# Attention in a four-layer kernel: the running maxima placed along a concave line, and the second one of a place put behind the values

## What is computed

```python
# 16 heads of 16 channels, 2048 queries and keys, causal
attn = jnp.einsum('bhqd,bhkd->bhqk', q, k) / math.sqrt(HEAD_DIM)
attn = attn + alibi_bias(seq_len, N_HEADS)[None] + causal_mask(seq_len)[None, None]
attn = jax.nn.softmax(attn, axis=-1)
y = jnp.einsum('bhqk,bhkd->bhqd', attn, v)
...
x = x + _L0_attn_ref(_layernorm(x, axis=-1), L0_attn_W_qkv, L0_attn_W_o)
...
x = x + _L1_attn_ref(_layernorm(x, axis=-1), L1_attn_Wq, ...)   # rotary instead of ALiBi
```

## Time and profile before

| | |
|---|---|
| Median of the runs shown | 1660.2 us |
| The profiled execution's own time | 1662.96 us |
| Span of its profile | 1661.2 us |
| Granted TensorE clock, mean of the span | 0.945 |
| Places of the first attention (0 to 319) | 233.0 to 674.1 us of the span |
| Places of the second attention | 1040.8 to 1496.9 us of the span |

### The profile page before, as it was taken

The page is one execution under the profiler, slowest core; times in us unless marked ns, Lnnn a source line. Parts: engine busy times, 40 slices in busy tenths (PEclk is TensorE's granted clock), DMA queues, the critical chain, the costliest instruction groups (busy, mean ns, idle before and its releaser), DMA issues. The chain is left out here.

```text
span 1661.2 us, 32231 instructions
## 1 busy us (share of the span) xinstructions
PE 1511.0 (91%) x13116; PEld 946.3 (57%) x13116; DVE 1242.6 (75%) x1741; ACT 945.3 (57%) x1893; POOL 207.6 (12%) x275
## 2 busy tenths in 40 slices
PE   2798888989999999999899698899999999998997
PEld 0687754444434445688688676544344344456887
DVE  7765457888898883576589887677788988735897
ACT  5454334757768887565344322456577688863442
POOL 0243000000000000157000033000000001220000
PEclk9899968999999999999999898789799999999999
DMA  6000869000000000200100067841110000000000
GB/s 218 26 0 9 176 169 130 25 21 25 15 14 14 2 2 2 77 1 1 39 1 1 1 138 205 104 59 45 39 33 25 13 12 2 2 1 1 13 13 26
DMA packets 38195, 70.58 MB, mean 42 GB/s; under 512 B 5490, under 2 KB 13298, under 8 KB 37236
## 3 DMA queue, kind: packets, MB, share of 16 engines
q1 hardware_dynamic: 38052, 68.58, 18.4%
HBM read 48.90 MB, written 22.15 MB: 43 GB/s over the span
## 5 line engine op out<-in xcount | busy, mean ns | idle before, releaser
L1362 DVE TENSOR_REDUCE l_att_maxima<-psum 128x2 f32<-128x1024 f32 (+3 forms) x640 | 664.8, 1063 | 137.1 <-PE psum L1154 128.6
L1547 ACT ACTIVATE l_att_probs<-psum 128x512 f32<-128x512 f32 (+3 forms) x1280 | 603.6, 533 | 263.4 <-PE psum L1184 242.7
L1201 PE MATMUL psum<-l_att_probs,l_att_v 128*17 128x256 f32 (+2 forms) x4608 | 352.7, 383 | 0.5
L1184 PE MATMUL psum<-l_att_qt,l_kt 51*128 51x512 f32 (+6 forms) x1280 | 319.6, 461 | 6.6 <-ACT l_att_probs L1547 6.6
L1154 PE MATMUL psum<-l_kt,l_att_qt 59*128 59x512 f32 (+7 forms) x1280 | 287.6, 427 | 4.6 <-DVE l_att_maxima L1362 3.0
L1184 PEld LDWEIGHTS psum<-l_att_qt,l_kt 59*128 59x128 f32 (+1 forms) x1280 | 138.0, 192 | 156.1 <-ACT l_att_probs L1547 146.1
L1201 PEld LDWEIGHTS psum<-l_att_probs,l_att_v 128*17 128x17 f32 x4608 | 81.9, 96 | 143.1 <-issue 92.2
L1154 PEld LDWEIGHTS psum<-l_kt,l_att_qt 59*128 59x128 f32 (+1 forms) x1280 | 140.5, 202 | 18.8 <-DVE l_att_maxima L1362 17.4
L358 PE MATMUL psum<-xh,w_ternary 128*128 128x512 f32 x256 | 103.7, 405 | 21.0 <-PEq L165 16.3
L1502 POOL CAST l_att_crow<-l_att_cneg 128x16 bf16<-128x16 f32 x32 | 8.1, 252 | 802.4 <-DVE l_att_cneg L1372 802.4
L1151 PE MATMUL psum<-tri 64*128 64x128 bf16 x1024 | 89.2, 239 | 20.1 <-DVE l_att_maxima L1362 13.7
(11 more groups left out here) (209 smaller groups left out, 2507.0 us busy)
## 6 DMA issues: line engine op xcount, KB each, us to landing
l_kt<-qk_scratch SPq DMA_DIRECT2D x48, 256.0 KB, 10.2
qk_scratch<-l_att_kv_parts SPq DMA_DIRECT2D x22, 512.0 KB, 8.1
l_att_qt<-qk_scratch SPq DMA_DIRECT2D x168, 64.0 KB
qk_scratch<-y SPq DMA_DIRECT2D x10, 512.0 KB, 12.5
set_raw<-in_w_gu SPq DMA_DIRECT2D x2, 1024.0 KB, 7.0
y<-in_w_gu SPq DMA_DIRECT2D x1, 2048.0 KB, 7.6
y<-in_rope SPq DMA_DIRECT2D x8, 256.0 KB, 5.9
l_att_w_raw<-in_w_gu SPq DMA_DIRECT2D x4, 512.0 KB
```

The source lines that it names most:

```text
L1184: e.matmul(g.ps[:, score_bank(i), off:BLK], g.kt[rows_of(x), hp, kt * P:(kt + 1) * P], qt[rows_of(x), hp, off:BLK], start=u >= TPB, stop=True,
L1201: ins = e.matmul(g.ps[h * VW:h * VW + HD + 1, OB, lo:hi], g.v[:, kt, STEPS[st][1] * HG + h, :], pr[:, un % PB, h, lo:hi], start=u == 0 and ...
L1362: e.tensor_reduce(mp[:, st % 2, 2 * p:2 * p + 2, t, c], g.ps[:, bank:bank + 2, 0:w], AX.X, ALU.max).then_inc(s.mx, 1)
L1547: e.activation(pr[:, un % PB, h, off:BLK], g.ps[:, score_bank(i), off:BLK], ACT.Exp, scale=HD ** -0.5).then_inc(s.ex, 1)
```

## The change

The corners stay; what runs between them changes. Up to corner (16, 32) the straight lines are kept. From there on, `due` is the largest value that any chord between two of the later corners has at that place, that is, the concave line over the corners. It touches them at (16, 32), (24, 48), (88, 120), (184, 224) and (280, 320) and lies above the others. Between 24 and 88 it rises by 72 products in 64 places, between 88 and 184 by 104 in 96, and then by one for each place. So two products stand at places 16 to 23, then at 24, 32, 40, 48, 56, 64, 72, 80, 88, then at 100, 112, 124, 136, 148, 160, 172; all other places up to 279 have one. The number of places with two is 24, as before; the maxima run up to six products ahead of the old line.

The second part is `due_first`: the first product of a place stands where it stood, and a second one stands behind rows, output and values of that place. VectorE and ScalarE count the ring in the same new order. Sizes, banks, rings, waits and the places of rows, outputs and values are as before.

```diff
+        corners = [(maxima_place(st), mbase[st + 1]) for st in range(NS)]
+
         def due(p):
 
-            for st in range(NS):
-                end = maxima_place(st)
-                if p < end:
-                    begin = maxima_place(st - 1)
-                    return mbase[st] + -(-(mbase[st + 1] - mbase[st]) * (p - begin) // (end - begin))
-            return mbase[NS]
+            for (a, c), (b, d) in zip(corners[:NG - 1], corners[1:NG]):
+                if p < b:
+                    return c + -(-(d - c) * max(0, p - a) // (b - a))
+            late = corners[NG - 1:]
+            return max([-(-((d - c) * (p - a) + c * (b - a)) // (b - a)) for a, c in late for b, d in late if a <= p < b],
+                       default=mbase[NS])
+
+        def due_first(p):
+
+            return min(due(p) + 1, due(p + 1))
...
             for p in range(2 * TAIL):
                 scores(p // 2, p % 2)
-                for k in range(due(p), due(p + 1)):
+                for k in range(due(p), due_first(p)):
                     max_products(k)
...
                 if p >= LAG:
                     values((p - LAG) // 2, (p - LAG) % 2)
+                for k in range(due_first(p), due(p + 1)):
+                    max_products(k)
...
             for p in range(2 * TAIL):
-                for k in range(due(p), due(p + 1)):
+                for k in range(due(p), due_first(p)):
                     maxima(k)
...
+                for k in range(due_first(p), due(p + 1)):
+                    maxima(k)
```

More of the change, by code:

```diff
@@ L1559, in _ @@
                 exps(p // 2, p % 2)
-                ring += due(p + 1) - due(p)
+                ring += due_first(p) - due(p)
                 for st in range(1, NS):
@@ L1569, in _ @@
                         copy_out(st)
+                ring += due(p + 1) - due_first(p)
             for un in range(TAIL, UNITS):
```

## The result

The changed kernel took 1657.4 us in the median of 21 runs (1646.7 to 1669.2), the kernel before 1665.9 us in the median of its 21 runs. The ratio is 0.9945 with a 95% interval of 0.9923 to 0.9967: about 9 us or 0.55% faster, between 5.5 and 12.8 us. One run of the kernel before took 1825.6 us and counts as slow; the ratio compares fast runs alone. A second set of 12 runs on another chip gave 0.9940 (0.9909 to 0.9971), at a mean clock of 0.951 against 0.946.

The account below looks back on a forecast made before the run. TensorE was taken to end last outside the dense stretches, VectorE to set the pace inside them. From 1662.96 us, 2 x 6.4 spreading, 2 x 1.0 order and 8 clock gave 1640.2, adjusted toward the median to 1639 us; range 1630 to 1653 us.

Parts of the forecast that it names:

- The dense stretches: Places 72 to 87 and 160 to 183, where VectorE sets the pace; to fall from 28.7 and 37.0 us.
- The order alone is worth 1 us in places 16 to 23: Places 16 to 23: the second product behind the values evens VectorE's work, 1 us for each attention.
- I take 0.45, nearest to the streaming: Sixteen second products on the new line: 0.45 us each, near TensorE's streaming of about 0.42, 7.2 us in each attention.
- a place without values has room for it: Places 24, 32, 40, 56, 72, 88: a good part of the second product's 0.56 us wait is room TensorE has anyway.
- The upper bound of 0.94: Second products on the new line: at most 0.94 us each, the price where VectorE can't catch up.
- rival A: Second products on the new line cost 0.94 us each, so spreading wins nothing; about 1654 us, chance 0.12.
- spreading gives 13.6 - 7.2: Second products of the dense stretches, 13.6 us, cost 7.2 us once spread: 6.4 us back in each attention.
- at the other places the move behind the values costs nothing: Outside places 16 to 23: TensorE's work between two scores is the same, so nothing was counted.
- I count 8 of the 10.6 us as given back: Places 72 to 111 of the second attention: the clock recovers, returning 8 of 10.6 us.
- rival C: Places 24 to 183 of the second attention: back-to-back products make the clock fall repeatedly; about 1671 us, chance 0.05.
- the 0.35 of the prediction: Places 72 to 111 of the second attention: each microsecond at the lower clock level costs 0.35 us.
- The absolute figure: Whole kernel: 1639 us, from one execution's 1662.96 us less 22.8 us and half of its 2.8 us above the median.

Follow-up runs that it names:

- The order alone: Kernel before with its old straight lines, but the second product of a place put behind the values; ratio 0.9953.
- Short seconds: Two kernels: changed kernel from place 24 with only the second reduction, or only the second product, cut to 64 columns or keys; places 24 to 183 2.0 and 1.0 us less.
- short firsts: Changed kernel, but the first reduction of each pair in places 24 to 183 reads only 64 columns of each bank; these places 213.0 us against 218.3.
- both-short kernel: Changed kernel, but from place 24 on the second product and its reduction are both cut to 64; places 24 to 183 3.1 us less than 218.3.
- other places: Changed kernel with its 16 second products of places 24 to 183 moved to 30, 38, ... 86 and 94, 106, ... 178; ratio 0.9902, again 0.9907.
- chosen places: Changed kernel with its 16 second products moved to places with outputs and to 32, 48, 76, 96, 120, 144, 168; ratio 0.9901.
- no pairs: Changed kernel with the second products at 24, 32, 40, 56, 72, 88 moved to 30, 38, 46, 62, 78, 94; ratio 0.9891.
- giving TensorE more to do: Changed kernel with each score product of places 0 to 23 made three times into the same bank in both attentions; ratio 1.0141.

## Why the prediction was wrong

**What held.** The dense stretches are the dear ones, and thinned out TensorE is the busiest there: they shrank to 22.4 and 32.1 us, where 21.8 to 22.5 and about 32 had been named, with TensorE busy for 95% and 97% of them. The order alone is worth 1 us in places 16 to 23. Outside the two attentions the profiles have 764.0 and 762.9 us, so the gain lies inside them.

**The step that failed first: "I take 0.45, nearest to the streaming".** It measured (218.3 - 207.9) / 16 = 0.65 us. The sum had 7.2 us for the 16 and they cost 10.4: 3.2 us in each attention, 6.4 in all. I had the wait in the earlier trace rows and priced it at 0.03 us for each product, with the argument that a place without values has room for it. Places 40 and 41 show where that is wrong: place 40 stays at 0.97 us, and the wait falls in the next one, ahead of its values, which grows by 0.66. Short seconds (2.0 and 1.0 us) against short firsts (5.3) show that the handover carries a third to a half of the price; the both-short kernel leaves 7.3 us that shrinking the second product did not reach. The size is another matter than the place: over 32 to 71, with three of its five pairs back to back, a second product cost 0.44 us, what I had taken, since the places around give some of the wait back (40 to 47 grew by 0.46, of which 0.66 is place 41). The excess over 0.45 comes from the one at 24 (1.9 us) and the ten from 72 on (0.63). That 32 to 71 fits is luck, as the sum there left the handover out. The upper bound of 0.94 held in the mean, rival A's mechanism was right in kind, and its size lay halfway.

**A step that was right only by its end: "spreading gives 13.6 - 7.2".** It took the price in the dense stretch as a property of the density, and its 0.94 held a fall of the clock: without the 3.4 us at the lower level it is 0.75 to 0.79, as the 0.76 of the third stretch. The order alone brought it to 0.63 us in places 72 to 87. I had written that at the other places the move behind the values costs nothing and had counted nothing for it, and it brought 2.4 us in places 24 to 183 by itself, about 1 us of it at full clock. At full clock a second product costs about 0.77 us before and 0.65 after, so that 16 of them bring 1.9 us in each attention from line and order together, where the sum had 6.4.

**The step that failed second: "I count 8 of the 10.6 us as given back".** The falls of places 72 to 111 of the second attention did go in part (70.1 to 57.5 us). Against the first attention these places were 10.6 us longer and are 2.9 longer (57.5 against 54.6), so in this profile 7.7 of the 8 us came. But in both profiles of the changed kernel a new one of 10 us stands in places 56 to 63 (4.4 us of time), as rival C had it in kind, and the second profile fell in other places too. Over all runs the clock rose only from 0.948 to 0.952. That is 2 x 0.0041 x 1657 = 14 us less at the lower level, worth 4 to 5 us at the 0.27 us for each that the 58 runs of the kernel before show against each other, or the 0.35 of the prediction. (The 0.35 divides 10.6 us by 30 us at the lower level; the first attention has 3.4 of its own, and by the difference of 27.3 it is 0.39.) With line and order at full clock, 2 x (1.9 + 1.0) = 5.8, that makes 10 to 11 us, inside the measured interval of 5.5 to 12.8.

**And the base.** The absolute figure stood on one execution and a median of three runs: 1662.96 less 1.4, so 1661.6 us; 21 runs gave 1665.9. The 18.4 us between 1639 and 1657.4 are so 4.3 of base, 6.4 of the price, and the remaining 7.7 are the clock's: of the 8 us counted, the runs as a whole show next to nothing beyond what the price term already holds.

What takes the clock down stays open. All six kernels that keep the changed kernel's pairs back to back with the first reduction full show a fall of 7 to 17 us in places 32 to 71 of the second attention. The four others (other places, chosen places, no pairs, first reduction short) show none there, one of them in two profiles. Removing only those six pairs removed the fall and brought about 0.5%, some 2.4 us of it at full clock. That is an association, and three things stand against reading it as the cause. The chosen places keep one such pair, at 32, without a fall. The order alone has no second product in 24 to 71, and its second attention fell in the same places as the changed kernel's, from 58 on, for 13.7 us (0.88), while the kernel before, with the same program there, did not. And giving TensorE more to do did not bring the clock up in the second attention. For it speaks the other places' kernel. It has four pairs back to back of its own, and in both of its profiles the second attention falls for 10 us right behind the one at 130 (36.2 us for places 112 to 135 in the second profile, against 31.9 in the first attention); behind 106, 154 and 178 it does not.

## What to carry to other kernels

In a ring with two slots the place to look at is not the added product but the one after it: it waits for the first of the two to be read, and what stands behind it in that engine's order waits too. So price an insertion by when the first's slot has been read, against when the third could start, and try places with other work between them; which places are cheap is read from windows (0.3 to 0.5 us with an output beside, 0.8 to 1.0 elsewhere in places 88 to 159 here), since room without values was cheap in one stretch and dear in another. Where the clock moves between runs by as much as the change is worth, take the base from many runs and compare structure in windows at the same granted clock; a single fall of 3.4 us in the kernel before made two parts that add up look as if they overlapped.

## What had not been expected of the hardware

With TensorE recorded as busy for 49.7 of 49.7 us, the granted clock of places 0 to 15 in the second attention was 0.50, for the same added work that left it at 0.96 in the first attention. The two differ there in the rows of keys and queries (51 and 59) and in the transfers beside them (78 and 101 GB/s); which of it matters, or whether it is either, was not tried. A microsecond at the lower level cost 0.43 us in places 32 to 71 of the changed kernel: 59.1 us with 10.2 us at the lower level and 54.7 without.
